# Batch 0 of a four-stage fused block: V and the adapter's bias in banks of their own, the last rest on VectorE, another order in the opening

## The reference, cut to what matters

```python
x = x + diffusion(x, zX, zY, zR)            # Laplacian along rows and columns, reflected edges, + zR*x*(1-x)
# stage 2: masked pooling
scores = tanh(x @ W1 + b1) @ v              # (b, s)
p = softmax(where(mask, scores, -1e30)); x = x + (p @ x) / count
# stage 3: linear, per subject
x = x + x @ W[subject].T + b[subject]
# stage 4: adapter, per profile
z = relu(x @ Wd + bd)
x = x + layernorm(x + z @ Wu + bu) * g + b
```

## Time and profile before

| | us |
|---|---|
| median of 3 runs | 551.24 |
| lowest, highest | 550.38, 553.79 |
| profiled execution, device time | 550.72 |
| its span, first to last instruction | 548.9 |
| TensorE busy | 525.4 (96% of the span) |
| VectorE busy | 478.4 (87%) |
| ScalarE busy | 312.7 (57%) |
| GpSimd busy | 313.5 (57%) |

### The profile page before, as it was taken

The page is one execution under the profiler, slowest core; times in us unless marked ns, Lnnn a source line. Parts: engine busy times, 40 slices in busy tenths (PEclk is TensorE's granted clock), DMA queues, the critical chain, the costliest instruction groups (busy, mean ns, idle before and its releaser), DMA issues.

```text
span 548.9 us, 8952 instructions
## 1 busy us (share of the span) xinstructions
PE 525.4 (96%) x2793; PEld 411.0 (75%) x2793; DVE 478.4 (87%) x1197; ACT 312.7 (57%) x546; POOL 313.5 (57%) x283
## 2 busy tenths in 40 slices
PE   8997899999999999999999999999999999999995
PEld 3556677888588877888678885888778886888783
DVE  6659788999899997999899998999979998887677
ACT  5645564477536765567645775376654776344520
POOL 5146826596258935687275952589256872247231
PEclk9999999999999999999999999999999999999999
DMA  7984199567996599884997579974997856422652
GB/s 251 304 203 78 59 308 257 108 140 165 347 232 135 100 260 314 195 168 98 309 301 162 121 183 345 225 142 89 274 348 147 164 107 207 59 59 57 132 87 109
DMA packets 63941, 100.82 MB, mean 184 GB/s; under 512 B 10893, under 2 KB 16525, under 8 KB 63894
## 3 DMA queue, kind: packets, MB, share of 16 engines
q0 software_dynamic: 16544, 29.90, 33.2%
q1 hardware_dynamic: 38096, 53.54, 30.8%
q10 hardware_dynamic: 9254, 16.81, 8.1%
HBM read 67.43 MB, written 31.98 MB: 181 GB/s over the span
## 4 chain that ended last, share of the span: by engine, by line
PE 81%; DVE 11%; ACT 3%; issue 3%; POOL 1%; DVEq 0%; ACTq 0%; POOLq 0%
PE y L711 38%; PE front_ps L774 9%; PE front_ps L872 8%; PE front_ps L711 6%; PE front_ps L798 5%; PE front_ps L727 4%; PE front_ps L782 3%; PE front_ps L788 2%; DVE x2f L1628 2%; PE front_ps L819 2%; ACT zh L1192 2%; DVE pn L1575 1%; PE front_ps L846 1%; PE y L753 1%; PE front_ps L853 1%
## 5 line engine op out<-in xcount | busy, mean ns | idle before, releaser
L597 POOL TENSOR_TENSOR norm<-norm 128x1 f32<-128x1 f32 x64 | 51.3, 802 | 150.5 <-DVE norm L1655 149.6
L711 PE MATMUL y<-wth,x2h 128*128 128x512 f32 x256 | 103.9, 406 | 0.0
L711 PE MATMUL y<-wth,x2l 128*128 128x512 f32 x256 | 100.2, 392 | 0.0
L711 PE MATMUL y<-wtl,x2h 128*128 128x512 f32 x256 | 100.0, 390 | 0.0
L615 POOL TENSOR_TENSOR x2l<-x2f,x2h 128x1024 fp32r<-128x1024 f32 x32 | 76.9, 2404 | 15.1 <-ACT x2h L1063 14.4
L578 POOL TENSOR_TENSOR xd<-xn 128x1024 f32<-128x1024 f32 x28 | 55.7, 1989 | 36.1 <-DVE x L1484 19.8
L1628 DVE SCALAR_TENSOR_TENSOR x2f<-alb,small,front_ps 128x128 f32<-128x128 f32 x256 | 70.6, 343 | 1.3
L872 PE MATMUL front_ps<-th_pt,x 128*128 128x129 f32 x512 | 64.8, 278 | 2.7 <-DVE x2f L1628 1.8
L872 PEld LDWEIGHTS front_ps<-th_pt,x 128*128 128x128 f32 x512 | 62.0, 190 | 7.0 <-DVE x2f L1628 4.8
L604 POOL DMA_DIRECT2D out<-o_sb x58 | 57.6, 1072 | 8.0 <-ACT o_sb L1209 7.0
L1063 ACT ACTIVATE x2h<-x2f 128x1024 fp32r<-128x1024 f32 x32 | 34.0, 1062 | 47.1 <-DVE x2f L1628 47.1
(11 more groups left out here) (146 smaller groups left out, 1094.4 us busy)
## 6 DMA issues: line engine op xcount, KB each, us to landing
xn<-in_x SPq DMA_DIRECT2D x32, 512.0 KB, 7.7
out<-x ACTq DMA_DIRECT2D x58, 256.0 KB, 4.4
out<-o_sb POOLq DMA_DIRECT2D x58, 256.0 KB, 6.5
xu<-in_x SPq DMA_DIRECT2D x21, 512.0 KB, 8.9
xu<-in_x POOLq DMA_DIRECT2D x21, 512.0 KB, 8.0
wn_wd<-in_L_cond_weight SPq DMA_DIRECT2D x8, 1024.0 KB, 7.7
wn_wd<-in_L_cond_down_w SPq DMA_DIRECT2D x8, 256.0 KB, 6.9
up_row<-in_L_cond_up_b SPq DMA_DIRECT2D x8, 256.0 KB, 4.6
```

The costliest lines, as they stand in the source:

```text
L597: pool.tensor_tensor(rstd[:, r:r + 1], ve[:, r:r + 1], minus_half[:, :], ALU.pow).then_inc(rstd_ready, 1)
L711: ins = mm(dst, lhs, rhs, start=first and q == 0, stop=last and q == len(parts) - 1, skip_group_check=True)
```

## The change

- `v_bank(0)` and `bz_bank(0)` are in `pair_b` instead of `pair_a`; other batches as before. `down_through_w(0)` waits for `sb_read` 2 (the scores in `pair_b` have been read). For batch 0 the waits for `vl_ready` and `bz_ready` go from `transpose_p` to `transpose_alpha`.
- VectorE takes the rest of x2's last slice (k = 3) of batch 0: `last_first_rest_x2`. GpSimd's list has three `rest_x2` instead of four, with `rest_up` ahead of them and `start_sum` between the second and the third.
- `adapter_down` goes by pairs of halves for all batches: slices 0 and 1 for both halves, then slice 2 for both, then slice 3 for both.
- The orders of `opening` and `first` are changed on TensorE, ScalarE, VectorE and GpSimd.

```diff
+        def v_bank(n):
+            return (pair_a if n else pair_b)[:, 0:KD * P]
+        def bz_bank(n):
+            return (pair_a if n else pair_b)[:, 512:513]
 # GpSimd, first()
-                start_sum(0)
+                rest_up(0, 0)
                 rest_x2(0, 0, 0)
                 rest_x2(0, 0, 1)
+                start_sum(0)
                 rest_x2(0, 0, 2)
-                rest_x2(0, 0, 3)
-                rest_up(0, 0)
                 left_and_right(1, 3)
 # TensorE
 down_through_w(n):
+                if n == 0:
+                    pe.wait_ge(sb_read, 2)
 transpose_p(n, h):
-                pe.wait_ge(vl_ready, n + 1)
-                pe.wait_ge(bz_ready, n + 1)
+                if n:
+                    pe.wait_ge(vl_ready, n + 1)
+                    pe.wait_ge(bz_ready, n + 1)
 transpose_alpha(n):
+                if n == 0:
+                    pe.wait_ge(vl_ready, 1)
+                    pe.wait_ge(bz_ready, 1)
 adapter_down(n, q):
-                for h, ks in ((0, (0, 1, 2)), (1, (0, 1, 2)), (0, (3,)), (1, (3,))):
+                for h, ks in ((0, (0, 1)), (1, (0, 1)), (0, (2,)), (1, (2,)), (0, (3,)), (1, (3,))):
 opening():
                 fill(ys[0][:, :])
+                spread_scalars()
                 keep_warm()
-                spread_scalars()
...
+                sum_ends(2)
                 sum_sides(3)
-                sum_ends(2)
...
+                sum_sides(5)
                 transpose_x1(0, 0, 1)
-                sum_sides(5)
...
                 transpose_first_w(1)
+                transpose_first_w(2)
                 scores_by_row(0)
-                transpose_first_w(2)
+                down_through_w(0)
                 block_sums(0)
-                down_through_w(0)
+                transpose_p(0, 0)
                 transpose_first_w(3)
-                transpose_p(0, 0)
 first():
+                transpose_p(0, 1)
                 transpose_alpha(0)
-                transpose_p(0, 1)
...
+                clear_banks()
                 pool_blocks(0, 0, 3, (2,))
-                clear_banks()
...
+                linear(0, 0, 3)
                 adapter_up(0, 0, 2)
-                linear(0, 0, 3)
 # ScalarE: opening() has reflect(0, 3) ahead of seed_rows(1); first():
                 reflect(1, 0)
                 reflect(1, 1)
+                reflect(1, 2)
                 small_exps(0)
                 row_exps(0)
+                round_v(0)
                 scale_rows(1, 0)
-                round_v(0)
                 scale_rows(1, 1)
-                reflect(1, 2)
                 centre(1, 0)
                 keep_p(0, 0)
+                reflect(1, 3)
                 keep_p(0, 1)
                 keep_alpha(0)
+                scale_rows(1, 2)
                 round_first_w(3)
...
 # VectorE
+            def last_first_rest_x2():
+                dve.wait_ge(x2h_ready, KD)
+                dve.wait_ge(x2l_ready, KD - 1)
+                dve.tensor_tensor(x2l[0][:, KD - 1, :], x2f[:, (KD - 1) % 2, :],
+                                  x2h[0][:, KD - 1, :].bitcast(F32), ALU.subtract).then_inc(x2l_ready, 1)
 # opening(): make_ends() is first; add_sides(3) ahead of first_diffuse(0, 1);
 # add_identity(0) ahead of first_diffuse(0, 3). first():
                 maxima(0)
                 rest_first_w(0)
-                block_weights(0)
                 rest_first_w(1)
                 rest_first_w(2)
+                block_weights(0)
+                adapter_bias(0)
                 row_weights(0)
                 probabilities(0, 0)
-                rest_v(0)
-                adapter_bias(0)
                 add_around(1, 0)
                 probabilities(0, 1)
+                rest_v(0)
                 add_around(1, 1)
...
                 add_carry(0, 3, 1)
+                last_first_rest_x2()
                 times_x(1, 1)
+                add_around(1, 2)
                 diffuse(1, 1, 1)
-                add_around(1, 2)
+                rest_z(0, 0)
                 keep_x3(0, 0)
+                times_x(1, 2)
                 add_around(1, 3)
-                times_x(1, 2)
                 diffuse(1, 1, 2)
-                rest_z(0, 0)
-                keep_x3(0, 1)
                 times_x(1, 3)
                 diffuse(1, 1, 3)
                 rest_z(0, 1)
+                keep_x3(0, 1)
+                weigh_down(1)
```

More of the change, by code:

```diff
@@ L181, in build @@
         SN, ZG = cbank[:, 0:NJ], cbank[:, NJ:2 * NJ]
-        BZ = pair_a[:, 512:513]
+        def v_bank(n):
+            return (pair_a if n else pair_b)[:, 0:KD * P]
+        def bz_bank(n):
+            return (pair_a if n else pair_b)[:, 512:513]
         GROUPS = ((0, 3), (3, 6), (6, 8))
@@ L795, in down_through_w @@
                 pe.wait_ge(th_ready, 2 * n + 2)
+                if n == 0:
+                    pe.wait_ge(sb_read, 2)
                 for hb in range(KD):
                     for ob in range(KD):
-                        ins = mm(pair_a[:, blk(hb)], wn[:, ob, blk(hb)], wd[:, ob, :],
+                        ins = mm(v_bank(n)[:, blk(hb)], wn[:, ob, blk(hb)], wd[:, ob, :],
                                  start=ob == 0, stop=ob == KD - 1)
@@ L801, in down_through_w @@
                 pe.wait_ge(down_b_made, KD * n + KD)
-                mm(BZ, down_b[:, :], ones[:, 0:1], start=True, stop=True).then_inc(bz_ps, 1)
+                mm(bz_bank(n), down_b[:, :], ones[:, 0:1], start=True, stop=True).then_inc(bz_ps, 1)
             def block_sums(n):
@@ L1147, in round_v @@
                 wait_past(act, z_ps, 2 * n)
-                copy(vh[:, :, :], pair_a[:, 0:KD * P].rearrange("p (k q) -> p k q", k=KD)
+                copy(vh[:, :, :], v_bank(n).rearrange("p (k q) -> p k q", k=KD)
                      ).then_inc(vh_ready, 1)
@@ L1231, in opening @@
                 reflect(0, 2)
+                reflect(0, 3)
                 seed_rows(1)
                 seed_rows(2)
-                reflect(0, 3)
                 square(2)
@@ L1266, in first @@
                 round_x2(0, 0, 2)
+                centre(1, 1)
                 round_x2(0, 0, 3)
-                scale_rows(1, 2)
-                centre(1, 1)
-                reflect(1, 3)
+                scale_rows(1, 3)
                 seed(0, 0)
@@ L1273, in first @@
                 adapter_relu(0, 0)
-                scale_rows(1, 3)
                 adapter_relu(0, 1)
-                seed(0, 2)
                 centre(1, 2)
                 keep_x1t(1, 1, 0)
+                store_base(0, 0)
                 keep_x1t(1, 1, 1)
@@ L1281, in first @@
                 round_up(1, 1)
+                seed(0, 2)
+                hidden(1, 0)
                 keep_x1t(1, 1, 2)
                 keep_x1t(1, 1, 3)
+                seed(0, 3)
+                scale(0, 0)
                 store_base(0, 1)
-                hidden(1, 0)
-                scale(0, 0)
-                seed(0, 3)
                 hidden(1, 1)
-                store_base(0, 0)
             def steady(b, n, m, q):
@@ L1544, in rest_v @@
                 dve.wait_ge(vh_ready, n + 1)
-                dve.tensor_tensor(vl[:, :, :], pair_a[:, 0:KD * P].rearrange("p (k q) -> p k q", k=KD),
+                dve.tensor_tensor(vl[:, :, :], v_bank(n).rearrange("p (k q) -> p k q", k=KD),
                                   vh[:, :, :].bitcast(F32), ALU.subtract).then_inc(vl_ready, 1)
@@ L1583, in adapter_bias @@
                 wait_past(dve, zf_ready, 4 * n)
-                dve.tensor_tensor(bz[:, :], BZ, bd_col[:, :], ALU.add).then_inc(bz_ready, 1)
+                dve.tensor_tensor(bz[:, :], bz_bank(n), bd_col[:, :], ALU.add).then_inc(bz_ready, 1)
             def rest_w(n, part):
@@ L1684, in opening @@
             def opening():
+                make_ends()
                 write_table()
                 add_sides(0)
-                make_ends()
                 make_sides()
@@ L1693, in opening @@
                 first_diffuse(0, 0)
+                add_sides(3)
                 first_diffuse(0, 1)
-                add_sides(3)
                 first_diffuse(0, 2)
+                add_identity(0)
                 first_diffuse(0, 3)
-                add_identity(0)
                 weigh_down(0)
@@ L1729, in first @@
                 carry_products(0, 2)
+                rest_first_w(3)
                 carry_sums(0, 2)
-                rest_first_w(3)
                 add_carry(0, 2, 2)
                 add_carry(0, 2, 0)
+                carry_products(0, 3)
                 add_carry(0, 2, 1)
-                carry_products(0, 3)
                 carry_sums(0, 3)
@@ L1754, in first @@
                 add_identity(1)
-                weigh_down(1)
                 mask_scores(1, 0)
```

## The result

| | before | after |
|---|---|---|
| median, 21 runs each | 551.32 us | 553.15 us |
| ratio after/before | | 1.0031 (95%: 1.0020 to 1.0042) |
| profiled execution, its span | 550.72, 548.9 us | 553.68, 551.9 us |

The account below looks back on a forecast made before the run. TensorE bounds the steady stretch, VectorE 45 to 60 us. Running shift: -0.35 at the sums, +2.6 at the weights, +1.4 at linear, +0.95 after the last wait; 551.24 + 0.95 = 552.2 us, range 549.0 to 554.2.

Parts of the forecast that it names:

- Part 1, the opening: TensorE's opening: scalars' product earlier, 1.0 us idle, neighbour sums begin at 9.5 instead of 9.83, -0.35 us.
- The rival of the late clock: Opening: gap delays TensorE's clock rise, sums begin at 9.9 to 11.6, time 552.6 to 554.3 us; chance 0.18.
- Part 2, the collision: Softmax of batch 0: GpSimd's earlier left_and_right pair holds VectorE in maxima; row weights at 45.8 instead of 43.2, +2.6 us.
- E: The time TensorE ends spreading the scores: 34.64 us before, forecast 34.3.
- also across two GpSimd instructions back to back: Softmax: a VectorE instruction with two SBUF inputs stands still through both of GpSimd's left_and_right, 3.74 us together.
- V's banks: Batch 0, V in new banks: the 1.6 us wait for the bias goes, but VectorE is next late; worth 0 on the path.
- Part 3: End of x2 and down-projection in batch 0: linear at 68.8 against 67.35, +1.4, giving 1.2 back of 2.6 us.
- Part 4: Until batch 1's scores: TensorE's wait for the last diffusion goes, -0.47 us; later batches cost 0.
- the total of +0.95: Whole kernel: change after the last wait, added to the runs' median 551.24 for 552.2 us; chance 0.50.

Follow-up runs that it names:

- e2: Changed kernel with keep_warm ahead of spread_scalars again on TensorE in the opening; 551.80 us, ratio 1.0003.
- e4: Kernel before with spread_scalars ahead of keep_warm on TensorE and nothing else; 553.06 us, ratio 1.0017.
- e1: Changed kernel with small_exps(0) ahead of the three reflects of batch 1 on ScalarE; 552.98 us, ratio 1.0019.
- e3: Changed kernel with both edits: small_exps(0) ahead of batch 1's reflects, and keep_warm ahead of spread_scalars; 550.06 us, ratio 0.9981.
- e8: e3 with V and the bias back in pair_a and the transposes of p waiting for both again; 552.11 us, ratio 1.0010.
- e9: e3 with three products with no reader on TensorE between block_sums and transpose_p(0, 0); 549.40 us, ratio 0.9962.
- e10: e9 with clear_banks behind the last pool_blocks, carry_products(0, 3) behind add_carry(0, 2, 1), start_sum behind the third rest; 549.64 us, ratio 0.9960.
- e5: Kernel before with transpose_first_w(2) ahead of scores_by_row on TensorE and nothing else; 555.29 us, ratio 1.0067.
- e11: Changed kernel with four products with no reader while TensorE waits for p, nothing else; 552.97 us, ratio 1.0014.

## Why the prediction was right or wrong

**Part 1, the opening: the step that failed.** I took the sums to begin at 9.5, "two passes at 0.85 and one across the change end near 7.3", that is, with the clock rising at 7 us whatever TensorE did before. They began at 11.81, and the edit costs 1.35 us (e2) to 1.7 us (e4) in the medians, and 2.9 (e1 against e3) where the collision is gone. The rival of the late clock holds: its bound for the sums, 9.9 to 11.6, has two of the four profiles with the gap inside, at 10.25 and 11.19, and two just above, at 11.78 and 11.81. I gave it 0.18; it should have been the forecast. The arithmetic had the gap of 1.0 us right (1.01 measured) and priced what it does to the clock at nothing. The Trainium skill (TensorE: Matmul & The Clock Gate, Part 1) had pointed there: activity releases the throttle, at a point that varies from run to run. The traces agree in both: the passes are slow at first in every profile, and with the same opening lists the same four passes took 1.98 us in e3, e8 and e9, 2.22 in e10 and 2.75 in e2. The rest of the opening's reordering is a gain that I had not counted: with the gap closed the sums begin at 8.96 to 9.34 and not at 9.82, since make_ends no longer stands behind the table: VectorE has `sides` ready at 8.8 us in e3 and at 9.7 before.

**Part 2, the collision: right in place and kind, too large in size.** I forecast +2.95 us between E and the weights; it was +2.1. The mis-sized term is "also across two GpSimd instructions back to back": the changed kernel's L1541 (the old L1528) got through between the two (it lasted 1.61 us), and only L1548 (the old L1535) waited for the second (1.44), so the block was 2.7 us and not 3.55. (V's end, given as 41.1, is 41.2 by its own terms, E + 6.9; it came at 43.27, E + 6.7.) That the collision costs 1.7 us of time with the gap closed is shown by e3 against e2; in the changed kernel as it stands, taking it out brought 0.2 (e1). That transpose_first_w(2) triggers it is shown by e5.

**V's banks: "worth 0 on the path" was wrong.** e8 puts them at 2.0 us within the new order. What they are worth in the order of before was not tried.

**A cost that no step had.** One wait of 3 to 4.5 us for p replaces several short ones, and the clock falls inside it (e3 against e9). I had put V's banks and TensorE's waiting there at 0, because VectorE was the bound; the slow matmuls after it then made VectorE wait.

**Part 3: right.** From x2's last piece to linear it was 5.1 us before; I forecast 4.0 and it is 4.1. The new subtraction takes 1.23 us (1.25 forecast). start_sum ahead of the third rest, priced at 0.4, cost nothing: the rounding of slice 2 came only at 65.15, as clear_banks (0.96) and carry_products(0, 3) now stand in front of it.

**Part 4: right in the main.** The wait for the last diffusion is gone, and the steady batches are as before to 0.2 us; from linear to the end the span is 0.2 us shorter, where 0.47 was forecast.

**The sum.** The differences between the runs, in us:

| | medians | means |
|---|---|---|
| gap in the opening: after - e2 | 1.35 | 1.6 |
| the same without the collision: e1 - e3 | 2.9 | 2.5 |
| the same on the kernel before: e4 - before | 1.7 | 1.1 |
| collision, gap closed: e2 - e3 | 1.7 | 1.3 |
| collision, gap open: after - e1 | 0.2 | 0.4 |
| all the rest: e3 - before | -1.3 | -1.3 |

Gap and collision together cost 3.1 us, and with the rest that makes the +1.8 measured. How the 3.1 is shared between them depends on which is taken out first. The falls of the clock described at e9 may be the reason; that isn't shown. That the total of +0.95 came within 0.9 us is in part luck. At the stations the opening was 2.3 us later than forecast and the collision 0.9 us smaller, and the two errors have opposite signs.

## What to carry to other kernels

Before moving a small instruction earlier, ask which engine its result wakes and beside what that engine will then run: here a transposition moved ahead of the scores let GpSimd start beside VectorE's shortest and most critical instructions. An idle TensorE is not free even off the critical path, neither in the first microseconds nor in one wait of 3 us; a few products with no reader were worth 0.7 us and steadier runs in e9, though nothing that could be told in e11. Take out two causes both singly and together: here the two single edits would by the medians have put the loss at half of what the pair showed. Price an edit in the opening by what it does to the first rise of the clock, not by the idle time alone.

## What the runs showed of the hardware that was not expected

- A VectorE instruction that waits for GpSimd got through between two GpSimd instructions that ran back to back, in the changed kernel, e2, e5 and e11 (1.61 us and then about 1.44), while L1560 of the kernel before waits through both in six of the seven steady batches (3.09 us five times, 2.80 once). Both stand in the traces; what decides between them stays open.
- A gap of 0.8 to 1.0 us in TensorE's first 5 us went with sums that begin 0.4 to 2.0 us later than at 9.83, in four of four profiles.
- The granted clock fell to half inside an idle time of TensorE: 2.1 us into one of 3.07 (e3) and 1.7 us into one of 4.51 (after), for 6.8 us each. It also fell for 3.4 us at the end of an idle time of 1.14 us in e4, where the same 1.14 us in the kernel before went without a fall.
- In 84 runs of the kernel before that were timed beside the experiments the mean granted clock goes with the time: 21 runs at 0.986 to 0.989 took 553.5 to 553.9 us, and 63 at 0.993 to 0.998 took 550.4 to 551.6. The upper group of the first table is thus one of a lower clock; why a run falls into it stays open.
